# The gate's convolution taps: from VectorE to ScalarE copies and shifted accumulating DMAs

## The chip, the cores and the metric

The kernel runs on one core of a Trainium2 chip. The metric is device time in microseconds (us) of one execution, as the median of several runs. A core has TensorE (PE), VectorE (DVE), ScalarE (ACT), GpSimd (POOL) and SyncE (SP), each with a queue of its own that it works through in order, and 16 DMA engines that all queues share.

## The reference

A decoder layer on x of shape 16 x 256 x 256 (batch, tokens, width) with a context of the same shape. Three parts follow one another, each as `x = layernorm(x + part(x))`:

```python
# a: gated scan attention, K = 32 heads of H = 8, M = 4 angles, CK = 4 taps
z = x @ in_proj_w                                  # 256 -> 544 columns
z = causal_depthwise_conv(z, conv_w) + conv_b      # z[t] = sum of 4 taps over t-3..t
x_val, x_gate, s_raw = z[:, :256], silu(z[:, 256:512]), z[:, 512:]
p_w = exp(clip(scale * s_raw)) * time_weight
re, im = cumsum(p_w * poly(x_val) * cos/sin(x_val * theta)) / cumsum(p_w)
y = rms_normalised(re, im) @ W_re, W_im
out = (y * x_gate) @ out_proj_w
# b: autocorrelation attention over the context: spectra of q, k, v (DFT as matmuls),
#    correlation, top 5 of 256 lags, softmax, weighted roll of v, output product
# c: two low-rank expert branches: gelu router, softmax weights,
#    prod = (x V) * cumsum(x W) * weight, out = prod @ U, divided by the position
```

The convolution is causal: the output at token t takes the projection at t, t-1, t-2 and t-3 with one weight per channel and tap.

## The kernel before

The batch is worked in 8 chunks of 2 sequences (512 tokens). Channels lie on the 128 partitions and tokens along the free dimension, so a projection is a 128 x 512 float32 block in one PSUM bank. In each chunk part a has four such blocks z0 to z3: z0 and z1 are values, z2 and z3 the gate. Chunks overlap: while chunk i is in part a, chunk i-1 is in b and chunk i-2 or i-1 in c.

The order on each engine is written out by hand as a list of calls per engine, such as `a_project(1, 2)` (chunk 1, block 2), some 600 calls each for TensorE, ScalarE and VectorE. Every step has a semaphore that its followers wait for, through `Steps.tick` and `Steps.at`; `BANK_A`, `BANK_B` and `BANK_C` say which PSUM bank a step uses and `free_a` what must be done before the bank is taken again. In chunk 0 and at the start of chunk 1 there are also 34 `fold` steps, products of weights made once on TensorE and evacuated by ScalarE, with five PSUM banks in turn.

The steps around the change, by engine:

- TensorE: `a_project(i, j)` (L574) makes block j. z0, z2 and z3 share bank 1, so z3 waits until z2 has been read.
- ScalarE: `a_project(i, j)` (L1464) writes the last tap plus bias from PSUM to `zc`. `a_gate(i, h)` (L1502) applies SiLU to `zc[:, 2 + h]`. Behind it come `a_guard`, and for the eight units u of part a `a_angles` (abs, sin, cos: L1526, L1534, L1537), `a_turns` (L1519) and `a_squares` (L1553). `fold` is L1445.
- VectorE: `a_conv(i, j)` adds the other three taps with one instruction each, shifted by 1, 2 and 3 tokens (`a_tap`, L2501). Then, for each unit, `a_moments` (L2572), `a_fraction` (L2552) and `a_scan` (L2580).
- POOL: `a_accumulate(i, u)` (L2336) adds the squares of a unit to `acc` by an accumulating DMA, and `rstd` makes the layer norm factors.

`sq` holds the squares of two units (h = 0 and 1), each as two blocks of 512 tokens.

Of the kernel before, what the change touches and what calls it, by code (L numbers as in the profile page):

```python
# [87 lines left out]
def each(kinds, over):  # L88
# [10 lines left out]
VEC_A = Steps("vec_a", [("tap", j, t) for j in Z_ORDER for t in (2, 1, 0)] + [("stap", t) for t in (2, 1, 0)]  # L99
# [4 lines left out]
              + each("z", Z_ORDER) + each("turns abs cos sin sq", range(UNITS)) + NORM)  # L104
# [9 lines left out]
                        "w1", "w2", "w4", "w3a", "w3", "oa", "ob", "o"] + LAYER_NORM)  # L114
# [47 lines left out]
def is_first(i):  # L162

    return isinstance(i, int) and i == 0


def decoder_kernel(nc, x, ctx_in, out_proj, wq, bq, wk, bk, wv, bv, wo, bo, f_q, f_k, f_o, f_inv, v_fwd,
# [3 lines left out]
    with ctx:  # L171
# [69 lines left out]
        sq = sb("sq", [P, 2, 2, T])  # L241
        acc = sb("acc", [P, 2, 2, T])
# [67 lines left out]
        added = [sem(f"pool_a_add{h}") for h in range(2)]  # L310
        ready = sem("ready")
# [37 lines left out]
        def _(sp):  # L349
# [30 lines left out]
            load_x(1)  # L380
            load_ctx(1)
            load_ctx(2)
            load_x(2)
            load_residual(1)
            load_residual(2)
            load_x(3)
            load_x(4)
            store(0)
            load_residual(3)
            load_ctx(3)  # L390
            load_x(5)
            store(1)
            load_residual(4)
            store(2)
            load_x(6)
            load_ctx(4)
            load_ctx(5)
            load_residual(5)
            store(3)
            load_ctx(6)  # L400
            load_residual(6)
            load_x(7)
            store(4)
            load_ctx(7)
            load_residual(7)
# [23 lines left out]
        def _(pe):  # L429
# [53 lines left out]
            def free_a(i, *name):  # L483
# [331 lines left out]
            fold(11)  # L815
            a_sums(0, 1)
            fold(12)
# [4 lines left out]
            fold(17)  # L822
            a_sums(0, 2)
            a_sums(0, 3)
            fold(18)
            fold(19)
# [8 lines left out]
            fold(26)  # L835
            a_factor(0, 1)
            fold(27)
            a_transpose(1, 0)
            a_transpose(1, 1)
            a_out(0, 0)  # L840
            a_scores(1)
            a_out(0, 1)
            fold(28)
            a_project(1, 0)
            a_project(1, 1)
            fold(29)
            fold(30)
            fold(31)
            fold(32)
            fold(33)  # L850
            a_spread(1, 0)
# [5 lines left out]
            b_transform(0, "xf", 1)  # L857
            a_spread(1, 1)
            b_spectrum(0, "qa")
            a_project(1, 2)  # L860
            b_spectrum(0, "qb")
            b_spectrum(0, "ka")
            b_spectrum(0, "kb")
            b_spectrum(0, "va")
            b_spectrum(0, "vb")
            a_project(1, 3)
            a_sums(1, 0)
# [3 lines left out]
            a_sums(1, 1)  # L871
            b_back(0, 0)
            b_back(0, 1)
            b_out(0, 0)
            b_out(0, 1)
            a_sums(1, 2)
            a_sums(1, 3)
            b_transform(1, "cf", 0)
            b_transform(1, "cf", 1)
            c_transpose(0, 0)  # L880
            c_transpose(0, 1)
            a_squares(1)
            c_hidden(0, 0)
            c_hidden(0, 1)
            a_factor(1, 0)
            c_hidden(0, 2)
            a_factor(1, 1)
            a_transpose(2, 0)
            a_transpose(2, 1)
            a_out(1, 0)  # L890
            a_scores(2)
            a_out(1, 1)
            a_project(2, 0)
            c_hidden(0, 3)
            a_project(2, 1)
            c_logits(0)
            a_spread(2, 0)
            c_running(0, 0)
            c_turn(0)
            c_own(0, 0)  # L900
            b_transform(1, "xf", 0)
            b_transform(1, "xf", 1)
            a_spread(2, 1)
            a_project(2, 2)
# [2616 lines left out]
```

## Time and profile before

| | |
|---|---|
| median of 3 runs | 964.4 us (962.87 to 967.22) |
| the profiled execution | 964.8 us, span of its instructions 963.0 us |
| TensorE busy | 873.6 us (91%) |
| VectorE busy | 759.5 us (79%) |
| ScalarE busy | 545.6 us (57%) |
| POOL busy | 93.6 us (10%) |

The busy times come from one profiled execution; the engines run side by side, so they don't add up to the span. A row of the profile names the engine, the line of the kernel, the operation, the tile written and the tile read, the shape, and how often it ran. "Idle before" is time in which the engine stood in front of such an instruction, with the engine whose work ended the wait.

### The profile page before, as it was taken

To read this page: it belongs to the slowest core of one execution; us is meant where nothing else is said; L and a number is where in the kernel's file an instruction comes from. 1 tells how busy PE (TensorE), PEld (TensorE's weight loads), DVE (VectorE), ACT (ScalarE), POOL (GpSimd) and SP (SyncE) were. 2 spreads that over 40 slices of the span, in tenths; PEclk is the share of its full clock that TensorE was granted. 3 is DMA by queue.
4 is the path that set the end of the run, shared out by engine and by line. 5 is a ranking of instruction groups with operands and counts; after the bars stand their busy time and mean duration, and the time that the engine had idled before them with its cause. 6 is when DMAs were issued, how large, how long until landed. Compare 5 with 4: busy or idle time off the path is not lost.

```text
span 963.0 us, 10915 instructions
## 1 busy us (share of the span) xinstructions
PE 873.6 (91%) x3672; PEld 519.0 (54%) x3672; DVE 759.5 (79%) x1274; ACT 545.6 (57%) x886; POOL 93.6 (10%) x174
## 2 busy tenths in 40 slices
PE   3579937999999999999999999999999998997896
PEld 1136714464666466554765475546655575655345
DVE  5696899799988997899889997899898994264231
ACT  3584884775658384858385564857393645312310
POOL 2010002200220012000110021001200021001000
PEclk9779968999999999999999999999999999999898
DMA  9651006210611025102430061103410060000000
GB/s 293 131 96 36 22 13 119 66 46 1 126 50 44 0 47 100 52 1 44 88 110 1 0 124 53 44 1 63 90 45 0 1 132 22 0 1 23 0 1 22
DMA packets 41212, 50.77 MB, mean 53 GB/s; under 512 B 14843, under 2 KB 34374, under 8 KB 41158
## 3 DMA queue, kind: packets, MB, share of 16 engines
q0 software_dynamic: 7008, 25.21, 13.9%
q1 hardware_dynamic: 34006, 24.48, 8.9%
q8 instruction: 30, 0.49, 0.2%
q10 hardware_dynamic: 144, 0.39, 0.2%
q14 instruction: 24, 0.20, 0.1%
HBM read 20.68 MB, written 4.19 MB: 26 GB/s over the span
## 4 chain that ended last, share of the span: by engine, by line
PE 74%; DVE 12%; ACT 9%; issue 3%; POOL 1%; DMA 1%; ACTq 0%; SPq 0%; DVEq 0%; POOLq 0%
PE ps L790 12%; PE ps L762 11%; PE ps L771 10%; PE ps L651 6%; PE ps L591 5%; PE ps L728 4%; PE ps L574 4%; PE ps L436 3%; PE ps L621 3%; PE ps L705 3%; PE ps L695 3%; DVE zc L2501 2%; PE ps L635 2%; DVE sc L2580 2%; PE ps L737 1%
## 5 line engine op out<-in xcount | busy, mean ns | idle before, releaser
L2580 DVE TENSOR_TENSOR_SCAN sc<-mask,sc 128x1024 f32<-128x1024 bf16 x64 | 146.2, 2285 | 0.6
L771 PE MATMUL ps<-x2t,mv 128*128 128x512 f32 x256 | 121.8, 598 | 0.2
L762 PE MATMUL ps<-cum,mw 128*128 128x512 f32 x256 | 121.5, 597 | 0.1
L790 PE MATMUL ps<-up,prod 128*128 128x256 f32 x512 | 115.6, 381 | 1.0 <-DVE prod L2820 0.9
L790 PEld LDWEIGHTS ps<-up,prod 128*128 128x128 f32 x512 | 94.7, 190 | 21.3 <-issue 7.1
L1649 ACT ACTIVATE cs<-ps 128x512 f32<-128x512 f32 x64 | 38.1, 595 | 106.7 <-PE ps L762 106.7
L2336 POOL DMA_DIRECT2D acc<-sq x48 | 42.0, 876 | 568.6 <-ACT sq L1553 568.6
L2572 DVE TENSOR_TENSOR sc<-sc,g 128x1024 f32<-128x1024 f32 x64 | 77.3, 1208 | 8.7 <-ACT sc L1537 8.6
L2501 DVE SCALAR_TENSOR_TENSOR zc<-ps,cst,zc 128x510 f32<-128x510 f32 (+2 forms) x96 | 71.3, 743 | 13.6 <-ACT zc L1464 11.2
L762 PEld LDWEIGHTS ps<-cum,mw 128*128 128x128 f32 x256 | 47.4, 190 | 58.6 <-issue 56.6
L771 PEld LDWEIGHTS ps<-x2t,mv 128*128 128x128 f32 x256 | 47.3, 190 | 49.6 <-issue 42.4
L1553 ACT ACTIVATE sq<-sc 128x1024 f32<-128x1024 f32 x48 | 50.6, 1054 | 38.2 <-DMA acc<-sq 21.8
L574 PE MATMUL ps<-xt,win 128*128 128x512 f32 x128 | 65.1, 637 | 7.0 <-DVE zc L2501 7.0
L2812 DVE TENSOR_TENSOR cs<-cs,ps 128x512 f32<-128x512 f32 x64 | 43.5, 679 | 33.3 <-ACT cs L1649 21.0
L1400 ACT ACT_TABLE_LOAD x48 | 61.6, 1283 | 2.0 <-PEq L3508 1.2
L591 PE MATMUL ps<-sc,wy 64*64 64x512 f32 x512 | 62.6, 614 | 0.0
L728 PE MATMUL ps<-x2t,mr 128*128 128x512 f32 x128 | 59.7, 613 | 1.0 <-ACT x2t L1609 1.0
L2820 DVE TENSOR_TENSOR prod<-cs,ps 128x512 f32<-128x512 f32 x64 | 43.9, 685 | 14.8 <-PE ps L771 13.7
L1519 ACT ACTIVATE hq<-zc,cst 128x512 int32<-128x512 f32 x64 | 46.0, 721 | 5.9 <-DVE zc L2501 4.9
L2552 DVE SCALAR_TENSOR_TENSOR frac<-zc,cst,hq 128x512 f32<-128x512 f32 x64 | 47.3, 744 | 1.5 <-ACT hq L1519 1.2
L1537 ACT ACTIVATE sc<-hq,quarter 128x512 f32<-128x512 f32 x64 | 45.5, 711 | 0.0
L1534 ACT ACTIVATE sc<-frac 128x512 f32<-128x512 f32 x64 | 39.7, 620 | 7.6 <-PE ps L591 7.6
(261 smaller groups left out, 1470.9 us busy)
## 6 DMA issues: line engine op xcount, KB each, us to landing
acc<-sq POOLq DMA_DIRECT2D x48, 512.0 KB, 4.6
xa<-in_x_dram SPq DMA_DIRECT2D x8, 512.0 KB, 4.5
xs_a<-in_x_dram SPq DMA_DIRECT2D x8, 512.0 KB, 3.6
cin<-in_ctx_dram SPq DMA_DIRECT2D x8, 512.0 KB, 3.6
out_dram<-prod SPq DMA_DIRECT2D x8, 512.0 KB, 3.2
win<-in_in_proj_dram SPq DMA_DIRECT2D x1, 544.0 KB, 6.4
prod<-in_L_ffn_V_fwd_dram SPq DMA_DIRECT2D x2, 256.0 KB
prod<-in_L_ffn_W_fwd_dram SPq DMA_DIRECT2D x2, 256.0 KB
```

The source lines that it names most:

```text
L574: last = mm(o, win[:, t, j * P:(j + 1) * P], xt[:, t, :], start=(t == 0), stop=(t == DT - 1))
L591: last = mm(ps[dst, BANK_A[("Y", r)], :], wy[src, 1 - c, m, :], sc[src, (2 * m + h) % 4, c, :], start=(m == 0 and c == 0), stop=(m == M - ...
L651: last = mm(o[:, b * D:(b + 1) * D], spec[:, first + t, c:c + P], w[:, t, :], start=(t == 0), stop=(t == DT - 1 and not biased))
L728: last = mm(o, mr[:, t, br, r * P:(r + 1) * P], x2t[:, t, :], start=(t == 0), stop=(t == 1))
L762: last = mm(o, mw[:, t, br, c:c + P], cum[:, t, :], start=(t == 0), stop=(t == 1))
L771: last = mm(o, mv[:, t, br, c:c + P], x2t[:, t, :], start=(t == 0), stop=(t == 1))
L790: mm(d, prod[:, j, q * P:(q + 1) * P], up[:, j, :], start=(j == 0), stop=False)
L1400: act.preload_act_table_set(name)
L1553: A(dst, sc[:, u % 4, :, :], ACT.Square, scale=1.0 / math.sqrt(2.0 * HD * M))\
L2501: STT(o[:, :, s:L], z[:, :, 0:L - s], cw[:, j, tap:tap + 1], o[:, :, s:L], ALU.mult, ALU.add)\
L2572: TT(sc[:, s, :, :], sc[:, s, :, :], g[:, h, :].unsqueeze(1).broadcast_to([P, 2, T]), ALU.mult)\
L2580: V.tensor_tensor_scan(flat, mask[:, 0:2 * T], flat, 0.0, ALU.mult, ALU.add)\
```

## The change

The three earlier taps of z2 and z3 are no longer made by VectorE. ScalarE writes each scaled block from PSUM to a place in SBUF (`a_side`, three copies per block), and POOL issues an accumulating DMA for each (`a_join`) that adds it, shifted by 1, 2 or 3 tokens, to `zc`. Two of the three places are the halves of `sq`, the third is a new tile `extra`. Each join waits for the one before it on the same block; `a_gate` waits for the third. z0, z1 and the scores keep their taps on VectorE. The bank of z2 and z3 is free when ScalarE's last side copy is done. The call lists of TensorE, ScalarE, VectorE and POOL and the order of SP's loads and stores are new throughout; three semaphores of `b_apply` become one.

```diff
-VEC_A = Steps("vec_a", [("tap", j, t) for j in Z_ORDER for t in (2, 1, 0)] + ...
+VEC_A = Steps("vec_a", [("tap", j, t) for j in range(2) for t in (2, 1, 0)] + ...
...
-              + each("z", Z_ORDER) + each("turns abs cos sin sq", range(UNITS)) + NORM)
+              + each("z", Z_ORDER) + [("side", j, t) for j in (2, 3) for t in (2, 1, 0)] + each("turns abs cos sin sq", range(UNITS)) + NORM)
...
+        extra = sb("extra", [P, 2, T])
+        slot = [[sq[:, h, 0, :], sq[:, h, 1, :], extra[:, h, :]] for h in range(2)]
...
+        joined = [sem(f"pool_a_gate{h}") for h in range(2)]
...
+                elif kind == "z" and n[0] < 2:
+                    pe.wait_ge(*VEC_A.at(i, "tap", n[0], 0))
                 elif kind == "z":
-                    pe.wait_ge(*VEC_A.at(i, "tap", n[0], 0))
+                    pe.wait_ge(*ACT_A.at(i, "side", n[0], 0))
...
+            def a_side(i, j):
+                h = j - 2
+                if not is_first(i):
+                    act.wait_ge(added[h], 16 * (M - 1) * i)
+                    act.wait_ge(joined[h], 48 * i)
+                for n, t in enumerate((2, 1, 0)):
+                    A(slot[h][n], ps[:, BANK_A[("z", j)], :], ACT.Identity, scale=cw[:, j, t:t + 1])\
+                        .then_inc(*ACT_A.tick("side", j, t))
...
             def a_gate(i, h):
                 tables(SILU_SIN)
-                act.wait_ge(*VEC_A.at(i, "tap", 2 + h, 0))
+                act.wait_ge(joined[h], 48 * (i + 1))
...
                     dst = sq[:, h, :, :]
+                    if m == 1:
+                        act.wait_ge(joined[h], 48 * i + 32)
...
+            def a_join(i, j, n):
+                h, t = j - 2, 2 - n
+                s = TAPS - 1 - t
+                pool.wait_ge(*ACT_A.at(i, "side", j, t))
+                if n:
+                    pool.wait_ge(joined[h], 48 * i + 16 * n)
+                o = zc[:, j, :].rearrange("p (b l) -> p b l", b=SEQ)
+                z = slot[h][n].rearrange("p (b l) -> p b l", b=SEQ)
+                G.dma_start(o[:, :, s:L], z[:, :, 0:L - s], accum_op=ALU.add).then_inc(joined[h], 16)
```

POOL's list has, for each chunk, ahead of its accumulations:

```diff
+            a_join(0, 2, 0)
+            a_join(0, 3, 0)
+            a_join(0, 2, 1)
+            a_join(0, 3, 1)
+            a_join(0, 2, 2)
+            a_join(0, 3, 2)
             a_accumulate(0, 2)
```

ScalarE's list, chunk 0 around the gate:

```diff
             a_project(0, 2)
+            a_side(0, 2)
             a_project(0, 3)
+            a_side(0, 3)
+            a_gate(0, 0)
             fold(0)
-            a_gate(0, 0)
             a_gate(0, 1)
             a_guard(0)
             a_angles(0, 2)
             a_turns(0, 4)
             a_squares(0, 0)
             a_angles(0, 3)
+            fold(1)
             a_turns(0, 5)
-            a_squares(0, 1)
-            a_angles(0, 4)
-            fold(1)
             fold(2)
```

TensorE's list, the end of chunk 0, with `fold(23)` to `fold(26)` ahead of `a_squares(0)`:

```diff
             fold(22)
-            a_squares(0)
             fold(23)
             fold(24)
             fold(25)
+            fold(26)
+            a_squares(0)
+            fold(27)
+            fold(28)
+            fold(29)
             a_factor(0, 0)
```

ScalarE's list of chunk 1 around the gate is `a_side(1, 2)`, `a_project(1, 3)`, `a_side(1, 3)`, `b_spectrum(0, "vb")`, `b_exp(0)`, `b_wt(0)`, `a_gate(1, 0)`, `a_gate(1, 1)`. On VectorE `b_products(0)` to `b_mix(0)` now stand ahead of `a_moments(1, 2)`, and on TensorE `b_corr(0)`, `b_wt(0)` and `b_wf(0)` ahead of `a_sums(1, 0)`. On POOL `bias_parts()` stands ahead of `a_accumulate(1, 2)` and `rstd(0, 1)` ahead of `a_accumulate(1, 5)`.

## Rows read from the trace of the kernel before

**Rows 1.** The page's head and its busy time of each engine.
```profile
span 963.0 us, 10915 instructions
...
PE 873.6 (91%) x3672; PEld 519.0 (54%) x3672; DVE 759.5 (79%) x1274; ACT 545.6 (57%) x886; POOL 93.6 (10%) x174
```

**Rows 2.** Busy time by stretch: us, then PE, PEld, DVE, ACT, POOL.
```profile
core 0: us, PE busy (x) PEld busy (x) DVE busy (x) ACT busy (x) POOL busy (x), PEclk, DMA share, GB/s
0.00:103.00 103.00, 70.67 (x277) 38.59 (x278) 76.02 (x134) 59.79 (x110) 12.71 (x32) 0.87 0.57 130
103.00:190.00 87.00, 63.37 (x308) 38.76 (x308) 74.80 (x110) 59.30 (x92) 10.76 (x18) 0.88 0.27 61
...
276.00:798.00 522.00, 512.89 (x2219) 306.32 (x2218) 465.17 (x771) 329.84 (x531) 53.15 (x94) 1.00 0.22 50
798.00:963.00 165.00, 142.72 (x506) 85.55 (x506) 62.84 (x139) 43.05 (x74) 6.24 (x16) 0.94 0.03 10
```

**Rows 3.** Who PE waited for from 176 to 798 us.
```profile
PE ps L555 <- DVE zc L2609: 3.1, 4, 0.8
```

**Rows 4.** Who PE waited for up to 276 us.
```profile
PE ps L672 <- DVE cor L2713: 6.7, 1, 6.7
...
PE ps L663 <- ACT qkv L1584: 6.1, 1, 6.1
```

**Rows 5.** Groups of instructions: busy us, mean ns; idle before.
```profile
L762 PE MATMUL ps<-cum,mw 128*128 128x512 f32 x256 | 121.5, 597 | 0.1
...
L2501 DVE SCALAR_TENSOR_TENSOR zc<-ps,cst,zc 128x510 f32<-128x510 f32 (+2 forms) x96 | 71.3, 743 | 13.6 <-ACT zc L1464 11.2
...
L1400 ACT ACT_TABLE_LOAD x48 | 61.6, 1283 | 2.0 <-PEq L3508 1.2
...
L1464 ACT ACTIVATE zc<-ps,cst 128x512 f32<-128x512 f32 x32 | 24.6, 771 | 24.1 <-PE ps L574 24.0
...
L1649 ACT ACTIVATE cs<-ps 128x512 f32<-128x512 f32 x64 | 38.1, 595 | 106.7 <-PE ps L762 106.7
```

**Rows 6.** POOL in order of time, one of its 48 issues.
```profile
63.84 0.87 POOL L2336 DMA_DIRECT2D acc<-sq  x1 [1.96 <-ACT sq L1553]
```

**Rows 7.** DMA issues: KB each, median us from issue to landing.
```profile
acc<-sq POOLq DMA_DIRECT2D x48, 512.0 KB, 4.6
...
bp<-bp POOLq DMA_DIRECT2D x2, 16.0 KB, 1.7
```

**Rows 8.** ScalarE in order of time, chunk 0.
```profile
30.19 0.76 ACT L1464 ACTIVATE zc<-ps,cst 128x512 f32<-128x512 f32 x1
41.21 0.78 ACT L1464 ACTIVATE zc<-ps,cst 128x512 f32<-128x512 f32 x1 [10.27 <-PE ps L574]
...
44.37 0.63 ACT L1502 ACTIVATE zc<-zc 128x512 f32<-128x512 f32 x1 [1.60 <-DVE zc L2501]
...
50.35 0.72 ACT L1519 ACTIVATE hq<-zc,cst 128x512 int32<-128x512 f32 x1
...
53.58 0.63 ACT L1445 ACTIVATE qkv<-ps 128x256 f32<-128x256 f32 x2
```

**Rows 9.** VectorE in order of time, chunk 0.
```profile
35.13 2.29 DVE L2501 SCALAR_TENSOR_TENSOR zc<-ps,cst,zc 128x510 f32<-128x510 f32 x3
...
46.99 1.22 DVE L2572 TENSOR_TENSOR sc<-sc,g 128x1024 f32<-128x1024 f32 x1 [2.65 <-ACT sc L1537]
```

**Rows 10.** TensorE in order of time, chunk 0.
```profile
37.47 3.70 PE L574 MATMUL ps<-xt,win 128*128 128x512 f32 x4 [6.60 <-DVE zc L2501]
...
53.99 0.69 PE L453 MATMUL ps<-cst,qkv 128*128 128x128 f32 x2 [9.70 <-ACT qkv L1445]
```

**Rows 11.** Short stretches: clock, DMA share and GB/s stand last.
```profile
36.00:40.00 4.00, 2.53 (x3) 1.18 (x4) 1.38 (x2) 0.00 (x0) 0.00 (x0) 0.50 0.48 138
40.00:44.00 4.00, 4.00 (x27) 1.53 (x26) 1.90 (x3) 1.56 (x3) 0.00 (x0) 0.88 0.00 0
54.00:88.00 34.00, 34.00 (x146) 18.87 (x147) 28.48 (x44) 22.33 (x42) 5.41 (x6) 0.94 0.49 93
```

More of the change, by code:

```diff
@@ L927, in _ @@
             c_running(0, 5)
+            b_wt(1)
+            a_sums(2, 0)
             c_spread(0, 5)
@@ L998, in _ @@
             c_own(1, 4)
[L999 removed]
+            b_wt(2)
             c_running(1, 5)
@@ L1705, in _ @@
             fold(6)
+            a_squares(0, 1)
+            a_angles(0, 4)
+            fold(7)
+            fold(8)
             a_turns(0, 6)
@@ L1713, in _ @@
             a_squares(0, 3)
-            a_angles(0, 6)
-            a_squares(0, 4)
             fold(10)
@@ L1718, in _ @@
             fold(12)
+            a_angles(0, 6)
+            a_squares(0, 4)
+            fold(13)
             a_angles(0, 7)
+            fold(14)
             a_squares(0, 5)
+            fold(15)
             a_squares(0, 6)
-            fold(13)
-            fold(14)
-            fold(15)
-            a_squares(0, 7)
             fold(16)
             fold(17)
+            a_squares(0, 7)
             fold(18)
@@ L1765, in _ @@
             a_project(1, 2)
-            b_spectrum(0, "qb")
-            b_spectrum(0, "ka")
-            b_spectrum(0, "kb")
+            a_side(1, 2)
             a_project(1, 3)
+            a_side(1, 3)
+            b_spectrum(0, "vb")
+            b_exp(0)
+            b_wt(0)
             a_gate(1, 0)
@@ L1922, in _ @@
             a_turns(3, 5)
+            c_tile(1, 5)
             a_squares(3, 1)
+            a_angles(3, 4)
+            b_wt(2)
             c_tile(1, 6)
-            c_tile(1, 7)
-            b_back(2, 0)
-            a_angles(3, 4)
             a_turns(3, 6)
@@ L2344, in _ @@
             rstd(0, 0, VEC_A, POOL_A)
+            a_join(1, 2, 0)
+            a_join(1, 3, 0)
+            a_join(1, 2, 1)
+            a_join(1, 3, 1)
+            a_join(1, 2, 2)
+            a_join(1, 3, 2)
+            bias_parts()
             a_accumulate(1, 2)
@@ L2350, in _ @@
             a_accumulate(1, 7)
-            rstd(0, 1, VEC_B, POOL_B)
             rstd(1, 0, VEC_A, POOL_A)
-            bias_parts()
+            a_join(2, 2, 0)
+            a_join(2, 3, 0)
+            a_join(2, 2, 1)
+            a_join(2, 3, 1)
+            a_join(2, 2, 2)
+            a_join(2, 3, 2)
             a_accumulate(2, 2)
@@ L2362, in _ @@
             rstd(2, 0, VEC_A, POOL_A)
+            a_join(3, 2, 0)
+            a_join(3, 3, 0)
+            a_join(3, 2, 1)
+            a_join(3, 3, 1)
+            a_join(3, 2, 2)
+            a_join(3, 3, 2)
             a_accumulate(3, 2)
@@ L2890, in _ @@
             a_scan(1, 0)
+            b_products(0)
+            b_heads(0)
             a_moments(1, 1)
+            b_topk(0)
+            b_weight(0)
             a_fraction(1, 3)
             a_scan(1, 1)
-            a_conv(1, 2)
-            b_products(0)
-            a_conv(1, 3)
-            b_heads(0)
+            b_apply(0)
+            b_mix(0)
+            b_fold(1, "cf")
             a_moments(1, 2)
@@ L2909, in _ @@
             a_moments(1, 5)
-            b_apply(0)
+            b_residual(0, 0)
+            b_residual(0, 1)
             a_fraction(1, 7)
-            b_mix(0)
             a_scan(1, 5)
@@ L3233, in _ @@
             c_split(4)
-            a_poly(6, 1)
-            a_moments(6, 0)
-            a_fraction(6, 2)
             a_scan(6, 0)
+            c_scale(4, 0)
+            c_prod(4, 0)
+            b_apply(5)
+            c_scale(4, 1)
+            c_prod(4, 1)
+            b_mix(5)
+            c_scale(4, 2)
+            c_prod(4, 2)
+            c_scale(4, 3)
             a_moments(6, 1)
```

1073 lines of the change are left out of this document (539 added, 534 removed).

## The prediction

> **What bounds the kernel now.** I read the page's busy times first, then stretches of the span, then the lists of waits, then chunk 0 instruction by instruction. TensorE is busy for 873.6 of 963.0 us; VectorE follows with 759.5, ScalarE has 545.6 and POOL 93.6 [rows 1]. The average hides three stages. From 276 to 798 us, five of the eight chunks, TensorE works 512.9 of 522 us: 9.1 us of idle time is everything a relieved VectorE could give back there. The end, 798 to 963 us, holds no convolution at all. The beginning is where TensorE has time to lose: 32.3 us idle up to 103 us and 23.6 us from 103 to 190 us [rows 2]. In the saturated stretch the longest of TensorE's waits for another engine is 3.1 us in four pieces, for VectorE's gate product (L2609); that wait is the shape of the chain, not VectorE's load [rows 3]. In chunk 1 it waits 6.7 us for the top-k weights and 6.1 us for a spectrum copy: both belong to part b of chunk 0 [rows 4].
>
> **What the change removes.** Eight chunks times two gate columns times three taps are 48 of the 96 instructions of L2501, at 743 ns each: 35.7 us off VectorE, 4.5 us per chunk [rows 5]. In their place ScalarE makes 48 scaled copies of PSUM. The nearest rows are 771 ns (PSUM with scale and bias, L1464) and 595 ns (a plain copy, L1649); the new ones have a scale of their own per partition, so I take 0.75 us, 36 us in all, less the four table loads of 1.28 us that the new order drops (I counted 44 changes of table in it instead of 48) [rows 5]. ScalarE comes to about 576 us of 963 and stays far from full. POOL issues 48 more DMAs at 0.87 us, 42 us more on an engine that is 10% busy [rows 1, 6].
>
> **The new wait.** The three joins of a column add to the same bytes, so each waits on POOL until the one before has landed, and SiLU (`a_gate`) waits on ScalarE for all three. ScalarE is a queue: behind the gate stand `a_guard` and `a_angles(i, 2)`, and behind those VectorE's products and scans of units 2 to 7. No row shows a join. A join moves 256 KB as 256 pieces of about 1 KB. The nearest rows are the 512 KB accumulation, 4.6 us from issue to landing, and the 16 KB copy, 1.7 us [rows 7]. A straight line between them gives 3.1 us for 256 KB; for the shorter pieces I take 3.5 us, and keep 1.7 and 4.6 as ends. The same 512 KB accumulation tests a rule of the Trainium skill (DMA: Bandwidth & Descriptors, Anatomy of one DMA — SWDGE (gpsimd) path): 2.0 us plus bytes over 436 GB/s. That rule would have it land in 3.2 us, where the trace has 4.6; for a join the rule gives an estimate of 2.6 us, and the sum below would then come to 961.0 us.
>
> **Chunk 0, step by step.** Before: ScalarE copies z2 at 30.19 us and then stands until 41.21, because z3's matmul on TensorE starts only at 37.47, when VectorE has done z2's taps (35.13 plus 2.29) [rows 8, 9, 10]. After: z2's copy ends at 30.96, the three side copies at 31.7, 32.5 and 33.2. z3's matmul starts at 33.2, 4.3 us earlier. It took 3.70 us at a granted clock of 0.50 [rows 10, 11], that is at 1.2 GHz; with the same time it ends at 36.9. z3's copy ends at 37.7, its first side copy at 38.4. Here the gain is used up. POOL issues `a_join(0, 3, 0)` at 38.4 and, because its queue is in order, `a_join(0, 2, 1)` only behind it at 39.3. Column 3 is complete at 38.4 + 3 x 3.5 = 48.9 us, column 2 at 39.3 + 2 x 3.5 = 46.3. The weight loads that fill the DMA engines until 40 us (share 0.48 from 36 to 40, then 0.00) [rows 11] touch only the first join of column 2, which has slack. So the second gate starts at 48.9 instead of 44.37 [rows 8], and VectorE, which has nothing else in its list, takes up unit 2's product about 4.5 us later than its 46.99 [rows 9]. What TensorE sees is different: it stood until 53.99 for ScalarE's evacuation of fold 1, at 53.58 [rows 8, 10]. The new list has fold 1 one unit earlier, right where `a_turns(0, 5)` stood: 50.35 - 44.37 = 5.98 us behind the second gate's start [rows 8]. That puts it at 54.9, 1.3 us later than before. From 54 to 88 us TensorE has no idle time [rows 11], so this shift is passed on whole: **+1.3 us**. With landings of 1.7 us fold 1 would come at 49.5 (-4.1), with 4.6 us at 58.2 (+4.6).
>
> **The end of chunk 0.** VectorE's last scans come 4.5 us late, but the new TensorE order has four more folds (23 to 26) ahead of `a_squares(0)`; they cover the delay. In return only seven folds instead of eleven are left to fill the short waits of normalisation, gate and output. For that I take **+1 us** (0 to +3).
>
> **Chunk 1.** The gate is well covered: between the side copies and `a_gate(1, 0)` stand `b_exp(0)` and `b_wt(0)`, which wait for top-k and TensorE anyway. VectorE has 4.5 us less to do. But the new order puts all of `b_products` to `b_mix` of chunk 0 ahead of unit 2, so that TensorE meets the top-k chain with no sums of chunk 1 to put in between; the 6.7 and 6.1 us [rows 4] stay in one form or another, and the hidden layers of c, brought forward, fill as much later on. I set this to **0**, between -4.5 (all six taps were on the path) and +5 (the b chain delays the scans by its own length and is only half filled).
>
> **Chunks 2 to 7 and the end.** Against 9.1 us of idle time [rows 2] VectorE gains 4.5 us of room per chunk. A third of it back is **-3 us** (0 to -9). Between the last side copy and the gate the new lists have two to five copies of c's tiles, a top-k exponential or both. TensorE makes a tile's running product in 1.9 us (121.5 us for 64, L762 [rows 5]) and its own product in as long, about 4 us a tile, so most of a 10.5 us join chain lies under work ScalarE would have waited for anyway. Moved steps: `bias_parts` goes ahead of chunk 1's accumulations on POOL, and its folds are done by then; `rstd(0, 1)` goes ahead of three of them, with its cause also earlier; SP's loads are reordered, and no wait of TensorE in the saturated stretch is for a load; the renamed step of `b_apply` changes only semaphores. All these I cost at nothing; what covers the loads is that each of them is issued most of a chunk ahead, and an uncovered one would cost about what the other 512 KB transfer takes, 4.6 us [rows 7], once. After 798 us nothing of weight changes.
>
> **Sum.** 1.3 + 1 + 0 - 3 = -0.7 us on the profiled execution's 964.8 us (span 963.0 and 1.8 around it): 964.1. The median of the runs is 0.4 lower, 964.4; so I forecast **963.7 us**. What a measurement of this kernel can tell from no change is about 0.5%, 4.8 us: below 959.6 is faster, above 969.2 slower.
>
> **Rivals.** *The relief comes through (faster).* Joins land in 2 us: the second gate starts at 44.4, fold 1 comes at 50.4, 3.2 us earlier; the taps of chunk 1 were on the path (-4.5); -3 later on. That is -10.7, 953.7 us. For it: VectorE is nearly full from 103 us on [rows 2], and the two stalls of TensorE on a convolution tap go away [rows 10]. Against it: the only accumulating DMA on record takes 4.6 us. The Trainium skill's fit of 2.6 us (same page and section) leans to this side. *The gate starves TensorE (slower).* Joins take 4.6 us like the accumulation: fold 1 at 58.2 (+4.6), +1, and a chain of 13.8 us between first side copy and second gate no longer fits under about 8 us of tile copies; ScalarE stands 4 us or more, the tile copies behind the gate come late, and TensorE, whose next running product needs the bank, loses 1 us in each of six chunks; with the -3 this is +8.6, 973 us. It decides from landings of about 4.2 us on. For it: ScalarE has waited up to 10.27 us at one point of its queue before [rows 8], and the joins share POOL and the DMA engines with loads. Against it: half the bytes. *The copies hold the bank.* z3 must wait for ScalarE's last side copy of z2 instead of VectorE's last tap. In chunks 2 to 7 spectra stand between the two projections; I price it at nothing, at most 0.8 us per chunk where they don't suffice.
>
> **Chances.** Forecast (TensorE full, gains and the late fold cancel; its own range 960 to 969): 0.42. Relief: 0.31. Starved: 0.27. The range reaches to both rivals' values and cuts a tenth on each side: 953 to 975. Faster 0.31, same 0.42, slower 0.27.
>
> **What would show it.** In the profile after: 48 instructions of the tap line at about 743 ns and VectorE near 724 us; side copies near 0.75 us; joins landing in 3 to 4 us; in chunk 0 z3's matmul at 33 us and SiLU waiting on ScalarE for a DMA until 46 to 49 us; TensorE's long stand ending at 55 us; its idle time from 276 to 798 us at 4 to 8 us. The forecast is wrong if joins land under 2.5 or above 4.2 us, if chunk 1's idle time moves by more than 4 us, or if ScalarE's waits at the gate reach TensorE.

## The result and the profile after

The changed kernel takes **988.97 us** in the median of 4 runs (986.42 to 991.75), the kernel before 963.63 us (4 runs) in the same series. The ratio is 1.0255, 95% interval 1.0233 to 1.0278: 25 us slower. The forecast was 963.7 us, no change that could be measured, with a range of 953 to 975; the time lies outside it.

The page's head and busy times after, to be read beside [rows 1]:

```profile
span 984.5 us, 11007 instructions
...
PE 880.3 (89%) x3672; PEld 520.4 (53%) x3672; DVE 726.8 (74%) x1226; ACT 566.0 (57%) x930; POOL 159.3 (16%) x222
```

VectorE is relieved by 33 us, as intended, and TensorE does the same 3672 matmuls. The span is 21.5 us longer, and only GpSimd's share of it has grown, from 10% to 16%. The same stretches as [rows 2]:

```profile
core 0: us, PE busy (x) PEld busy (x) DVE busy (x) ACT busy (x) POOL busy (x), PEclk, DMA share, GB/s
0.00:103.00 103.00, 68.54 (x260) 36.28 (x261) 63.66 (x112) 58.05 (x105) 18.54 (x34) 0.85 0.69 150
103.00:190.00 87.00, 60.38 (x268) 36.56 (x268) 67.82 (x94) 58.56 (x93) 27.92 (x28) 0.86 0.36 67
...
276.00:798.00 522.00, 509.21 (x2204) 302.03 (x2203) 440.86 (x734) 341.80 (x555) 87.55 (x119) 1.00 0.32 63
```

In the first two stretches VectorE does 12.4 and 7.0 us less, more than the 4.5 us of taps that each chunk lost: it waits, and its work comes later. From 276 to 798 us TensorE's idle time is 12.8 us, where it was 9.1 us [rows 2]. The lists of waits say who waited for whom. ScalarE's largest new wait, over the whole span (us in total, times, longest):

```profile
ACT zc L1518 <- DMA zc<-extra: 28.3, 14, 9.1
```

VectorE's and TensorE's, the latter up to 276 us as [rows 4]:

```profile
DVE sc L2666 <- ACT sc L1553: 28.8, 10, 18.1
```

```profile
PE ps L596 <- DVE sc L2674: 8.6, 2, 6.5
PE ps L456 <- ACT cor L1450: 8.5, 1, 8.5
PE ps L456 <- ACT qkv L1450: 7.2, 1, 7.2
...
PE ps L579 <- ACT extra L1480: 5.8, 3, 2.9
```

This is one chain: the SiLU (L1518) waits for the third join; behind it in ScalarE's queue are the angles (L1553), for which VectorE's products (L2666) wait, and the folds (L1450), for which TensorE waits. The new list has `fold(0)` between the two SiLUs, where the old one had it ahead of both, so TensorE stands twice. Chunk 0 in order of time shows it, to be read beside [rows 8, 9, 10]:

```profile
31.87 1.39 POOL L2371 DMA_DIRECT2D zc<-sq  x1 [24.21 <-ACT sq L1480]
...
32.76 3.78 PE L579 MATMUL ps<-xt,win 128*128 128x512 f32 x4 [2.91 <-ACT extra L1480]
...
38.24 2.46 POOL L2371 DMA_DIRECT2D zc<-sq  x2 [4.99 <-ACT sq L1480]
...
42.63 1.19 POOL L2371 DMA_DIRECT2D zc<-sq  x1 [1.92 <-DMA zc<-sq]
44.30 1.19 POOL L2371 DMA_DIRECT2D zc<-extra  x1 [0.48 <-issue]
46.97 1.19 POOL L2371 DMA_DIRECT2D zc<-extra  x1 [1.47 <-DMA zc<-sq]
48.20 0.63 ACT L1518 ACTIVATE zc<-zc 128x512 f32<-128x512 f32 x1 [9.11 <-DMA zc<-extra]
...
49.15 0.69 PE L456 MATMUL ps<-cst,qkv 128*128 128x128 f32 x2 [8.53 <-ACT cor L1450]
50.76 0.63 ACT L1518 ACTIVATE zc<-zc 128x512 f32<-128x512 f32 x1 [1.67 <-DMA zc<-extra]
...
53.38 1.23 DVE L2666 TENSOR_TENSOR sc<-sc,g 128x1024 f32<-128x1024 f32 x1 [18.13 <-ACT sc L1553]
...
57.02 0.69 PE L456 MATMUL ps<-cst,qkv 128*128 128x128 f32 x2 [7.19 <-ACT qkv L1450]
```

The joins of the second gate block go out at 38.24, 42.63 and 46.97, the second and third each as soon as the one before has landed; the block is whole at 50.76. TensorE stands 8.53 us for fold 0 and 7.19 us for fold 1, 15.7 us together, where it stood 9.70 us before [rows 10]. The issues of DMAs, answering [rows 7] (KB each, median us from issue to landing):

```profile
acc<-sq POOLq DMA_DIRECT2D x48, 512.0 KB, 4.5
...
zc<-sq POOLq DMA_DIRECT2D x16, 255.0 KB, 3.8
zc<-sq POOLq DMA_DIRECT2D x16, 254.0 KB, 4.6
zc<-extra POOLq DMA_DIRECT2D x16, 253.0 KB, 3.8
```

The landings are medians; the longest of the 48 joins took 6.4 us. And where the prediction's unknown prices came out, by instruction (ns shortest, median, longest):

```profile
L1480 ACT ACTIVATE sq<-ps,cst x32: 673/686/707, 30.9 to 761.9; 128x512 f32<-128x512 f32 x32
```

```profile
L2371 POOL DMA_DIRECT2D zc<-sq x32: 1192/1233/1718, 31.9 to 766.7; - x32
L2371 POOL DMA_DIRECT2D zc<-extra x16: 1192/1201/1211, 44.3 to 771.0; - x16
```

### The profile page after: what moved, and what is told of

It is laid out like the page before. It is cut to its first block, busy times and chain, and to the rows that moved or that the text cites. A ratio compares the mean times of both kernels' runs of the same rounds, so it can differ in the third digit from the quotient of the medians.

```text
span 984.5 us, 11007 instructions
## 1 busy us (share of the span) xinstructions
PE 880.3 (89%) x3672; PEld 520.4 (53%) x3672; DVE 726.8 (74%) x1226; ACT 566.0 (57%) x930; POOL 159.3 (16%) x222
## 4 chain that ended last, share of the span: by engine, by line
PE 66%; ACT 10%; DVE 9%; DMA 6%; issue 6%; POOL 2%; ACTq 0%; POOLq 0%; SPq 0%; DVEq 0%
PE ps L795 11%; PE ps L776 8%; PE ps L767 8%; PE ps L656 6%; PE ps L596 5%; PE ps L733 4%; DMA zc<-sq 4%; PE ps L710 3%; PE ps L626 3%; PE ps L439 3%; PE ps L700 3%; PE ps L579 3%; DMA zc<-extra 2%; ACT x L1672 2%; PE ps L640 1%
## 5 line engine op out<-in xcount | busy, mean ns | idle before, releaser
L2666 DVE TENSOR_TENSOR sc<-sc,g 128x1024 f32<-128x1024 f32 x64 | 77.3, 1208 | 28.9 <-ACT sc L1553 28.8
L2371 POOL DMA_DIRECT2D zc<-sq x32 | 39.2, 1343 | 264.5 <-ACT sq L1480 247.7
L596 PE MATMUL ps<-sc,wy 64*64 64x512 f32 x512 | 65.8, 638 | 8.6 <-DVE sc L2674 8.6
L1553 ACT ACTIVATE sc<-hq,quarter 128x512 f32<-128x512 f32 x64 | 45.5, 711 | 0.0
L1542 ACT ACTIVATE hq<-frac 128x512 f32<-128x512 f32 x64 | 39.9, 623 | 9.2 <-DVE frac L2646 9.1
```

Of the source, the lines that this page charges most:

```text
L596: last = mm(ps[dst, BANK_A[("Y", r)], :], wy[src, 1 - c, m, :], sc[src, (2 * m + h) % 4, c, :], start=(m == 0 and c == 0), stop=(m == M - ...
L2666: TT(sc[:, s, :, :], sc[:, s, :, :], g[:, h, :].unsqueeze(1).broadcast_to([P, 2, T]), ALU.mult)\
```

## The experiments

The first four ask one question from both sides: is it ScalarE's stand in front of the SiLU, the traffic of the joins, or the new order (the expectations call it the searched order)? In the kernels without joins and without VectorE's taps the gate is made from its last tap alone (the three earlier ones are left out), which is said here once for those whose expectation doesn't say it. The experiments ran in four series, each with the kernel before beside them (964.43, 963.48, 964.18 and 963.24 us; 963.63 us beside the changed kernel), so by my estimate a difference between kernels of two series is uncertain by about 1 us more.

**e1, no joins.** The changed kernel without `a_join` and without the two waits for `joined` in `a_side` and `a_squares`; the SiLU waits only for ScalarE's own copy.

```
-            a_join(i, 2, 0) ... a_join(i, 3, 2)      # POOL's list, all chunks
-                act.wait_ge(joined[h], 48 * (i + 1))
+                act.wait_ge(*ACT_A.at(i, "z", 2 + h))
```

> The changed kernel with its new lists and ScalarE's 48 side copies, but without the 48 joins: the three earlier taps of the gate are left out, and SiLU waits for ScalarE's own copy alone. Theory A (ScalarE stands at SiLU for the join chain, and what is queued behind it comes late): most of the 25 us comes back, 960 to 968 us. Theory B (the searched order itself is worse: folds and part b of chunk 0 moved ahead of chunk 1's sums): little comes back, 980 us or more. Theory C (the load of 48 more ScalarE copies): little comes back either, since the copies stay.

**e2, late gate.** Complete; ScalarE's list alone is changed, in each chunk:

```
-            a_gate(i, 0)
-            a_gate(i, 1)
...
             a_angles(i, 7)
+            a_gate(i, 0)
+            a_gate(i, 1)
```

> The changed kernel with a_gate(i, 0) and a_gate(i, 1) moved on ScalarE to just behind a_angles(i, 7), the same table set, so that nothing is queued behind the wait for the joins; joins, copies and all else stay. Theory A: as with the joins left out, 960 to 970 us. Theory B and C: 980 us or more. If the joins cost by their DMA traffic or POOL time rather than by the wait, this stays near 985 while the run without joins is fast.

**e3, old order.** The mechanism (side copies, joins, `extra`) put into the kernel before, whose order stays; the side copies stand right behind `a_project(i, 2)` and `a_project(i, 3)`, the joins ahead of `a_accumulate(i, 2)`.

```
             a_project(i, 2)
+            a_side(i, 2)
             a_project(i, 3)
+            a_side(i, 3)
...
-            a_conv(i, 2)                             # VectorE
-            a_conv(i, 3)
```

> The kernel before, its own lists unchanged but for the mechanism: a_side behind each a_project(i, 2) and (i, 3), the gate's a_conv dropped from VectorE, the joins on POOL ahead of each chunk's accumulations. Theory A: the gate stands in some chunks directly behind the copies, where the stall is worst: 990 us or more. Theory B: the new order is what costs, so with the old one 965 to 975 us.

**e4, old order, late gate.** e3 with e2's edit.

> The same with the old lists, and SiLU moved to behind a_angles(i, 7). Theory A: near the kernel before or a little below, 955 to 965 us, since VectorE has 36 us less to do and ScalarE no stall. Theory B: equal to the run of the old order with the early gate.

Measured, against 964.43 us for the kernel before: e1 968.02 us (ratio 1.0025, interval 1.0008 to 1.0042), e2 968.24 us (1.0038, 1.0024 to 1.0053), e3 1030.6 us (1.0672, 1.0644 to 1.07), e4 968.37 us (1.0035, 1.002 to 1.005). Moving two instructions of ScalarE per chunk takes 21 us off the changed kernel and 62 us off e3. With the gate late, the 48 joins cost nothing that can be measured (e2 and e1 agree), although POOL and the DMA engines do all of their work in e2. So it is not contention. With the early gate the new order is 42 us faster than the old one (e3). e4 missed its range (955 to 965 us): something else costs there. ScalarE's wait at the SiLU in e3:

```profile
ACT zc L1518 <- DMA zc<-extra: 58.1, 14, 9.6
```

It was 28.3 us in the changed kernel, and e2's and e4's lists of waits have none. 28.3 us less wait, 20.7 us less time (e2); 58.1 us less wait, 62.2 us less time (e4 against e3). And in e3 TensorE waits for what stands behind the SiLU:

```profile
PE ps L668 <- ACT qkv L1602: 27.4, 2, 17.7
PE ps L767 <- ACT cs L1667: 20.9, 6, 7.7
PE ps L456 <- ACT qkv L1450: 19.2, 1, 19.2
```

What this left open: 4 us over the kernel before, with VectorE relieved. The next four take the parts singly.

**e5, the late gate in the kernel before.** e2's edit, nothing else.

> The kernel before with nothing changed but the place of the two SiLUs on ScalarE: behind the last angles of their chunk, as in the old order with late gates (968.4 us against 964.4). No joins, no side copies, all taps on VectorE. It says what the late place costs by itself. If the 4 us that are left over the kernel before come from the late place (chunk's end later, a product that waits for it), it gives 967 to 970 us. If they come from the 48 side copies (48 times 0.69 us, 33 us more on ScalarE) and the joins, it gives 962 to 965 us. If ScalarE's waits for VectorE's taps in front of the SiLU cost something already before (10.3 us idle in chunk 0, [rows 8]), it gives under 962 us.

**e6, VectorE's relief alone.** The kernel before without `a_conv(i, 2)` and `a_conv(i, 3)`, nothing in their place; SiLU and the next user of the bank wait for ScalarE's copy instead of VectorE's last tap.

> The kernel before in its old order, with the gate's three earlier taps left out (48 instructions of VectorE, 35.7 us): no side copies and no joins in their place, so the gate is computed from its last tap alone. It prices VectorE's relief alone. Theory one, VectorE is not what bounds the chunks from the second on, and its relief is worth at most chunk 0's few microseconds: 956 to 962 us. Theory two, the relief is worth nothing, since TensorE's own work and ScalarE set every step: 963 to 965 us. Theory three, VectorE's time counts in each chunk (the 3.1 us of TensorE's waits for it and the queue behind it): 940 to 955 us. If it is well under 964 us, the late-gate kernels' 968 us holds a price of ScalarE's side copies of as much more.

**e7, the order alone.** The changed kernel's order with the 48 taps on VectorE.

```
-            a_side(i, j)                             # ScalarE
-            a_join(i, j, n)                          # POOL
+            a_conv(i, 2)                             # VectorE, e.g. behind a_scan(0, 1)
+            a_conv(i, 3)
```

> The order of the changed kernel on all engines and queues, but the gate's 48 taps made by VectorE again (put into its list near where the old list had them), no side copies and no joins. It prices the searched order alone. If the order costs nothing, 962 to 966 us; if the order is what leaves 4 us in the changed kernel without joins (968.0 us), 967 to 971 us; if the order fits only the new mechanism, whose VectorE list has no room for the taps, 972 to 985 us. It can't give the 989 us of the changed kernel if the joins' chain is the cause.

**e8, late gate in chunk 0 alone.** e2's edit for i = 0.

> The changed kernel, complete, with the two SiLUs of chunk 0 alone moved behind that chunk's last angles on ScalarE; in chunks 1 to 7 they stay where the change put them. It says where the 21 us arise. If each chunk's stop in front of the SiLU costs its own share, chunk 0's part comes back (5 to 12 us by the time at equal TensorE work, where the changed kernel was 6 us behind at 119 us and the late-gate one 5 to 8 us ahead) and the rest stays: 975 to 984 us. If only the shift of chunk 0 made all later chunks late: 967 to 971 us. If the later stops take back what chunk 0 gives: 985 to 990 us.

Measured, against 963.48 us: e5 961.98 us (0.998, 0.9964 to 0.9997), e6 949.74 us (0.9847, 0.9826 to 0.9869), e7 1013.44 us (1.0503, 1.0479 to 1.0528), e8 976.56 us (1.012, 1.0085 to 1.0154).

e6 is worth more than theory one allowed (8 us): leaving out these taps takes 13.7 us off, the shorter hold of the bank included. So the late-gate kernels, at 968 us, give all of it back and 4 us more: something of some 18 us was still hidden in them. The late gate is not it (e5). e7 shows that the new order goes with the mechanism: with the taps back on VectorE it is 50 us slower than the old order, 28 us above its highest range, and TensorE's largest wait in total is its projection's for a tap (7.0 us in the kernel before):

```profile
PE ps L577 <- DVE zc L2527: 23.4, 7, 7.5
```

The places of the taps in that list are mine, and no run shows how much better ones would give, so e7 doesn't price the order at its best. e8 puts 12.4 of the 21 us on chunk 0.

**e9, side copies without joins, old order.** e4 without `a_join`.

> The old order with the gates late, the side copies on ScalarE and no joins, so the gate's three earlier taps are left out. With both, this order took 968.4 us; with neither, and the gates early, 949.7 us. It splits these 18.7 us. If ScalarE's 48 side copies cost it (33 us of ScalarE, in its queue between the evacuation of a gate tile and what TensorE waits for): 964 to 969 us. If the joins cost it (48 transfers, and POOL's issue before the accumulations that ScalarE and VectorE wait for): 948 to 952 us. In the new order the joins were worth nothing once the gates did not wait for them (968.0 against 968.2 us), which speaks for the side copies.

**e10, neither, new order.** e1 without `a_side`.

> The changed kernel with neither joins nor side copies (the gate's three earlier taps left out), in its own order with the early gates. With side copies alone it took 968.0 us. If the side copies cost in this order what they cost in the old one: 948 to 953 us. If this order is made for them, so that their place costs nothing, and what it lacks is the order itself: 964 to 968 us.

**e11, small joins.** The changed kernel with

```
-                G.dma_start(o[:, :, s:L], z[:, :, 0:L - s], accum_op=ALU.add).then_inc(joined[h], 16)
+                G.dma_start(o[:, :, s:s + 32], z[:, :, 0:32], accum_op=ALU.add).then_inc(joined[h], 16)
```

> The changed kernel with its 48 joins, each of which adds 32 of the 256 positions of each of the two sequences (the rest of the earlier taps is left out): the same issues, semaphores and order, an eighth of the bytes (32 KB for 254 KB). ScalarE's stop is three landings and three issues in a row per tile. If a landing follows the bytes, it falls from 4.4 us to 2 us or less and the stop by half: 972 to 979 us. If most of a landing and its issue is a fixed price, it stays over 3 us: 982 to 988 us.

**e12, the taps later.** The kernel before, complete; only the lists of chunk 0:

```
             fold(14)                                 # TensorE
+            a_project(0, 3)                          # was behind fold(0)
...
             fold(12)                                 # ScalarE
+            a_project(0, 3)                          # was behind a_project(0, 2)
...
             a_squares(0, 7)
+            a_gate(0, 0)                             # were behind fold(0)
+            a_gate(0, 1)
...
             a_scan(0, 3)                             # VectorE
+            a_conv(0, 2)                             # both were behind a_scan(0, 1)
...
             a_scan(0, 6)
+            a_conv(0, 3)
```

> The kernel before, complete, with VectorE making all taps and no side copies or joins; only chunk 0's order is changed: the gate's second projection (matmul and evacuation) goes behind fold 14 on TensorE and fold 12 on ScalarE, the taps of the gate's tiles behind the scans of units 3 and 6 on VectorE, the two SiLUs behind the last square. If the relief of VectorE is worth something only because chunk 0's scans come earlier (the curve of the kernel without these taps is 9.4 us ahead at 20 us of TensorE's work and 11.6 us at the end of chunk 1), moving the taps out of their way gives most of chunk 0's part: 953 to 959 us. If the taps only move the delay to another place: 962 to 966 us. If the late gate holds up the end of chunk 0: 967 to 972 us.

Measured, against 964.18 us: e9 968.27 us (1.0046, 1.0031 to 1.006), e10 961.73 us (0.9973, 0.9957 to 0.9988), e11 977.12 us (1.0129, 1.0105 to 1.0153), e12 **954.58 us** (0.9898, 0.9876 to 0.9921).

e9 is as slow as e4: the hidden 18.5 us are ScalarE's side copies (968.27 against e6's 949.74), the joins again nothing. In the new order the copies cost 6.3 us (968.02 against 961.73): they hurt less there, in an order that without them is 12 us slower than the old one (961.73 against 949.74). e10 falls between its two ranges. e11 has the same issues and semaphores as the changed kernel with an eighth of the bytes:

```profile
zc<-sq POOLq DMA_DIRECT2D x32, 32.0 KB, 2.8
```

```profile
ACT zc L1518 <- DMA zc<-extra: 9.5, 4, 6.5
```

The first row is of its DMA issues, the second of ScalarE's waits: 9.5 us in 4 waits, down from 28.3 in 14. Landings are 1.0 to 1.8 us shorter, and the kernel is 11.9 us faster: the time follows the length of the chain. An eighth of the bytes still takes 2.8 us to land, so most of a landing does not go by the bytes.

**e13, half of the side copies elsewhere.** e9 with the copies of the second gate block behind the angles of unit 3.

```
             a_project(i, 3)
-            a_side(i, 3)
...
             a_angles(i, 3)
+            a_side(i, 3)
```

> The old order with the gates late and the side copies of both gate tiles but no joins (968.3 us), with one edit: the three copies of the second gate tile stand behind the angles of unit 3 in each chunk instead of right behind that tile's evacuation. As many copies, another place. If the place costs the 18.5 us over the kernel with neither copies nor joins (949.7 us), because six copies in a row hold the angles of unit 2 and what follows: 956 to 962 us. If their number costs it, wherever they stand: 966 to 970 us. If TensorE then waits for bank 1: over 970 us.

**e14, a third of them.** e9 with one copy per block, `enumerate((0,))` for `enumerate((2, 1, 0))` in `a_side`.

> The same kernel (968.3 us) with one side copy for each gate tile in place of three: 16 copies for 48, in the same places, 11 us of ScalarE for 33 us. If each copy costs by its time, a third of the 18.5 us stays: 954 to 958 us. If it is the first copy in the chain evacuation, copies, second gate matmul that counts, most stays: 962 to 967 us. If only the long row of six costs: 948 to 952 us.

**e15, late gate in chunks 0 to 2.** e2's edit for i = 0, 1, 2.

> The changed kernel, complete, with the gates of chunks 0, 1 and 2 late and those of chunks 3 to 7 early. With chunk 0 alone it took 976.6 us, with all eight 968.2 us. If the stops in chunks 1 and 2 cost the 8 us that were left: 967 to 970 us. If the five later chunks share them evenly with these two (1.2 us each): 973 to 975 us.

Measured, against 963.24 us: e13 967.66 us (1.0046, 1.0026 to 1.0066), e14 953.08 us (0.9911, 0.9884 to 0.9938), e15 975.25 us (1.0108, 1.0071 to 1.0144; three runs at 975.0 to 976.3 and one at 968.34).

e13 equals e9: this move of half of the copies changes nothing. e14 is 15 us faster, between two of its ranges: the number of copies counts. By the median a third of them costs 3.3 of the 18.5 us, less than its share; but e14's runs fall apart, five at 951.5 to 953.6 us with a mean granted clock of 0.969 to 0.975 and two at 959.5 and 959.9 us with 0.965 and 0.966, and by these two it would be 10 us. e9 from 276 to 798 us, and e14:

```profile
276.00:798.00 522.00, 509.64 (x2204) 302.72 (x2203) 441.83 (x735) 341.77 (x552) 50.55 (x88) 1.00 0.22 50
```

```profile
276.00:798.00 522.00, 511.54 (x2217) 305.58 (x2216) 442.33 (x730) 333.93 (x536) 51.12 (x89) 1.00 0.22 49
```

ScalarE is busy for 65% of this stretch in e9 and yet not free: TensorE's idle time is 12.4 us against 10.5 us. To see where each kernel loses, I took from each trace the start of the last matmul of part c's output product (the one that adds the bias, L791 before, L796 after) in chunks 0, 2, 4 and 7. Start before, and the others' difference to it, in us:

| kernel | chunk 0 | 2 | 4 | 7 |
|---|---|---|---|---|
| before | 262.2 | 468.6 | 681.2 | 953.3 |
| changed | +19.3 | +21.6 | +23.0 | +21.5 |
| e8, late gate in chunk 0 | +9.9 | +12.2 | +13.3 | +10.8 |
| e15, in chunks 0 to 2 | +6.0 | +8.4 | +12.1 | +10.7 |
| e2, in all | +5.3 | +6.6 | +5.9 | +3.4 |
| e10, new order, neither | -4.8 | -4.2 | -4.9 | -6.1 |
| e6, old order, neither | -11.9 | -12.6 | -14.0 | -15.1 |
| e14, one copy | -10.1 | -10.1 | -11.3 | -11.8 |
| e9, three copies | -2.1 | -0.4 | +1.9 | +1.5 |
| e12, taps later | -9.8 | -9.9 | -11.3 | -11.3 |

The changed kernel's loss is there when chunk 0 leaves part c. The output product of part a, which comes earlier, says in which chunk it arises (start of its first matmul, L621 before, L626 after):

| kernel | chunk 0 | 1 | 2 |
|---|---|---|---|
| before | 88.5 | 178.5 | 276.3 |
| changed | +7.9 | +20.3 | +20.1 |
| e8, late gate in chunk 0 | -3.5 | +9.6 | +10.7 |
| e2, in all | -6.6 | +9.1 | +6.1 |
| e10, new order, neither | -10.2 | -0.5 | -4.0 |
| e6, old order, neither | -9.4 | -11.6 | -11.9 |

Without copies and joins the two orders are level in chunk 0 (e10 and e6), and the new one is 11.1 us behind by chunk 1's product and 7.9 us by chunk 2's: its price arises in chunk 1. The orders place other work differently too, so a single point can be off by some microseconds.

e8, e15 and e2 share one TensorE order, so their rows compare directly. Chunk 0's stop costs 9.4 us at once and 10.7 us at the end. Those of chunks 1 and 2 cost 3.9 us at the first point of part c, but e15 and e8 end alike. The traces put this down to TensorE's clock and not to the stops. In the profiled execution of e15 the granted clock is at its lower level (1.2 GHz) for 3.4 us from 488.8 us, and again from 598.0 and from 809.6 us; between 200 and 860 us e8's and e2's have no such stretch. e15, then e8:

```profile
486.00:494.00 8.00, 6.81 (x29) 4.76 (x30) 5.59 (x15) 2.88 (x7) 1.56 (x4) 0.79 0.19 66
```

```profile
486.00:494.00 8.00, 6.53 (x41) 4.01 (x34) 4.26 (x8) 4.35 (x9) 0.00 (x0) 1.00 0.20 67
```

Just before it falls TensorE has stood for 0.23, 0.78 and 0.31 us; in e8 it stands at the same places for as long, and the clock stays. From chunk 2's point to chunk 7's e15 loses 3.7 us on e8. Its four runs point the same way: three with a mean granted clock of 0.956 to 0.958 take 975.0 to 976.3 us, the fourth, with 0.965, 968.34 us, which is e2's time. So e15 against e2 (7.0 us by medians) does not price the stops of chunks 3 to 7. ScalarE's wait at the SiLU in e15 is

```profile
ACT zc L1518 <- DMA zc<-extra: 8.8, 9, 1.5
```

and e8 against e2, neither with a lower clock there, goes from 5.6 us at chunk 2's point to 7.4 at chunk 7's: by these two traces the later stops cost about 2 us.

## Why the prediction was wrong

**What held.** The removal: 48 instructions off VectorE, 726.8 us for the 724 forecast. The side copies: 0.69 us for 0.75. In chunk 0 z3's matmul at 32.76 us for 33.2, fold 1 following the second SiLU by 5.9 us for 5.98. The mechanism was among the rivals, "the gate starves TensorE", with a chance of 0.27 and a price of 973 us.

**The account.** By medians, each step one difference between two kernels: the taps left out -13.7 us (e6), the new order without copies +12.0 (e10 against e6), the side copies in it +6.3 (e1 against e10), the joins as transfers, with the gate moved late, +0.2 (e2 against e1), the early SiLU +20.7 (changed against e2). They add up to +25.5 (measured +25.3) because each starts where the last ended, so the sum proves nothing. The first two terms stand between kernels that nobody would run, so each is a difference on this path and not a constant of the hardware: in the old order the path reads -13.7, +18.5, +0.1, +62.2, and the new order then takes back 41.6.

**Chunk 0, "+1.3 us" and "+1 us".** This step failed. By chunk 0's output product the kernel is 7.9 us late, for the 2.3 forecast. The prediction named as standing behind the gate `a_guard` and `a_angles(i, 2)` and followed fold 1 alone; it left out fold 0, which the new list has between the two SiLUs. TensorE stands 15.7 us for the two folds, where the prediction had one stand to 55 us. e8, which moves these two SiLUs alone, has 4.3 us there and is 12.4 us faster:

```profile
44.91 0.44 PE L456 MATMUL ps<-cst,qkv 128*128 128x128 f32 x2 [4.32 <-ACT qkv L1450]
```

**Chunk 1, "The gate is well covered", "I set this to 0", and the later chunks, "most of a 10.5 us join chain lies under work ScalarE would have waited for anyway".** These steps failed too. The prediction followed the SiLU through the queue in chunk 0 alone and judged the other seven chunks by the calls that lie between. In the trace ScalarE stands in front of 14 of the 16 SiLUs. In chunk 1, where the kernel falls back by another 12.4 us for the 0 forecast, the two waits are 3.3 and 1.6 us:

```profile
143.37 0.63 ACT L1518 ACTIVATE zc<-zc 128x512 f32<-128x512 f32 x1 [3.33 <-DMA zc<-extra]
145.56 0.63 ACT L1518 ACTIVATE zc<-zc 128x512 f32<-128x512 f32 x1 [1.56 <-DMA zc<-extra]
```

The larger loss of chunk 1 belongs to the new order, which has the b chain ahead of unit 2 and no sums of chunk 1 to fill it, as the prediction said and priced at nothing: e10, with neither copies nor joins, falls back by 9.7 us in chunk 1, e6 in the old order gains 2.2. TensorE waits there for a scan, in the changed kernel and, shorter, in e10:

```profile
156.40 3.69 PE L596 MATMUL ps<-sc,wy 64*64 64x512 f32 x16 [6.52 <-DVE sc L2674]
```

```profile
136.37 2.63 PE L596 MATMUL ps<-sc,wy 64*64 64x512 f32 x16 [3.83 <-DVE sc L2607]
```

In the kernel before TensorE has no wait for a scan between 60 and 200 us. Behind chunk 1 the changed kernel loses 1.2 us more up to its end, for the -3 us forecast.

**The length of the chain.** I took 3.5 us a landing; they take 3.8 to 4.6 us. The second block's chain runs from 38.24 to 50.76, 12.5 us for the 10.5 forecast, and SiLU comes at 50.76 instead of 48.9. TensorE's stand ends at 57.02, where I had 55 and the kernel before 53.99 [rows 10]. POOL's issue of a join takes 1.2 us, not 0.87. The straight line between [rows 7]'s two transfers put a join's landing too low: half the bytes land hardly sooner. My own threshold for the starving rival was a landing of "about 4.2 us"; chunk 0's chain just reached it (12.5 us for three), the median landing of all 48 joins, 3.8 us, did not. Nor did this size decide the side: in e11 the joins land in 2.8 us, under the 3.5 forecast, and it is still 13 us slower than the kernel before. The Trainium skill's fit (DMA: Bandwidth & Descriptors, Anatomy of one DMA — SWDGE (gpsimd) path) would have a join land in an estimated 2.6 us; the trace does not agree, with 3.8 to 4.6, nor does e11 for 32 KB, where the fit gives an estimated 2.1 and the row 2.8.

**"ScalarE comes to about 576 us and stays far from full."** True in busy time (566.0), wrong in price: I set the copies to nothing. They cost 6.3 us in the new order and 18.5 in the old one. TensorE hangs on ScalarE's evacuations in a strict order, and each copy ahead of one delays it; 57% is an average over moments in which it waits for TensorE and moments in which TensorE waits for it. Added up over the list of waits, TensorE waits 46.4 us for ScalarE in e9 and 30.3 us in e6, 16.1 us more, and the profiled span is 16.7 us longer at the same mean clock of 0.973. The largest parts are the fold in chunk 0, and the products of part b that wait for a copy of a spectrum's result; e9, then e6:

```profile
PE ps L456 <- ACT qkv L1450: 7.7, 1, 7.7
...
PE ps L656 <- ACT qkv L1599: 6.1, 5, 1.9
```

```profile
PE ps L453 <- ACT qkv L1447: 3.9, 1, 3.9
...
PE ps L653 <- ACT qkv L1586: 0.7, 2, 0.5
```

The rival "The copies hold the bank", priced at nothing, is a part of this. In the changed kernel TensorE's projection waits 5.8 us for a last side copy: 2.9 us in chunk 0, as forecast, but also 2.6 us in chunk 1, which the rival didn't look at. e10, where the bank is free after ScalarE's own copy, has 2.0 us of it, e9 3.1 and e6 1.0.

**The relief.** The -3 us of chunks 2 to 7 came near e6's row, which goes from -11.9 to -15.1, but by luck. The prediction took it from TensorE's idle time, and e6 has 11.2 us of that from 276 to 798 us, more than the 9.1 before:

```profile
276.00:798.00 522.00, 510.81 (x2204) 305.95 (x2215) 440.23 (x730) 329.40 (x530) 51.59 (x90) 1.00 0.22 49
```

Part of the gain is the clock. The profiled execution before has 3.4 us at the lower level from 587.1 us and again from 798.7, e6's has none from 200 to 875 us, and e12, with all taps on VectorE, gains the same 1.5 us between the points of chunks 2 and 4. The kernel before there:

```profile
585.00:593.00 8.00, 7.19 (x29) 4.67 (x30) 6.12 (x16) 2.79 (x6) 1.56 (x4) 0.79 0.20 68
```

What I missed is the beginning: 11.9 us by the time that chunk 0 is through. Nothing of it reached the changed kernel. I had compared two critical chains, taps before and joins after, and found them nearly as long; e6 and e12 show that neither has to be there. In e12 VectorE makes every tap, in other places, and is 9.8 us ahead at the same point: that gain was one of order, not of work. TensorE's two stands of [rows 10], 6.6 and 9.7 us, are gone; up to 103 us 7.9 us of waits for a scan stand in their place. In e12 the second gate projection runs at 50.35 us, when nobody waits for it, and VectorE's tap row comes after four scans:

```profile
42.83 2.28 DVE L2501 SCALAR_TENSOR_TENSOR zc<-ps,cst,zc 128x510 f32<-128x510 f32 x3
...
50.35 1.88 PE L574 MATMUL ps<-xt,win 128*128 128x512 f32 x4
```

**What stays open.** Why the granted clock falls in some executions and not in others of the same kernel: TensorE's stands just before are the same in e15 and e8. Which moved step of chunk 1 makes the new order's price there: no experiment took one back alone. And e13 shows only that this one move of the copies gains nothing, not that no place for them would.

## What to carry to other kernels

Before moving work to an idle engine, follow the first instruction that waits for the new result through its engine's queue in every chunk, and ask what is queued behind it: here two SiLUs that nobody needed yet held up everything, and moving them alone was worth 21 us. A low busy share doesn't make an engine's time free where another one hangs on its evacuations; price the added instructions with an experiment that leaves out the rest. And try the cheap reordering first: work that sits ahead of a critical row can be put behind it instead of being given away, which here is 1% faster than before (954.6 us) with no new mechanism, while the whole change cost 2.6%. Before a difference of a few microseconds is read as work or waiting, compare the granted clock of the two executions.

## What the runs showed of the hardware

- An accumulating DMA from SBUF to SBUF on POOL's queue lands in a median of 3.8 to 4.6 us at 253 to 255 KB, 4.5 at 512 KB and 2.8 at 32 KB: in these sizes most of a landing does not go by the bytes.
- POOL spends a median of 1.20 to 1.23 us on issuing one with 256 pieces, with 254 KB and with 32 KB alike, and 0.87 us on one of the 48 accumulations.
- 48 such transfers (12.5 MB more on the queue) cost this kernel nothing that can be measured, as long as nothing urgent waits for them (e4 and e9; e2 and e1).
- ScalarE's scaled copy of a 128x512 block out of PSUM takes 0.69 us, less than the 0.77 us of the one with scale and bias.
- TensorE's granted clock can fall to 1.2 GHz for 3.4 us in the middle of a stretch in which it is nearly always busy (e15 at 488.8 us, the kernel before at 587.1), and it can stay at 2.4 GHz in another execution whose TensorE stood for as long at the same places (e8 for e15). Three such stretches in e15 go with 3.7 us more than in e8.
